# A macaron block in one program: latent attention scores computed twice without transposes, key norms read into an own tensor, new order of the feed-forward phases

## What is computed

```python
x = x + 0.5 * ffn(layernorm(x))     # two layers: local attention (8 heads of 64, windows of 64) + gated MLP
x = x + attn(layernorm(x))          # latent attention, 16 heads of 8, causal
x = x + 0.5 * ffn(layernorm(x))

# attn
q_lat = jnp.einsum('bqhd,hdl->bhql', q, k_eff)
attn = jnp.einsum('bhql,bkl->bhqk', q_lat, c_kv) / sqrt(hs)
attn = jnp.where(causal[None, None], attn, -jnp.inf)
attn = jax.nn.softmax(attn, axis=-1)

# one ffn layer
q = l2norm(q) * qs; k = l2norm(k) * ksc
q, k = rotary_xpos(q, k)
o = local_attention(q, k, v)
x = x + o @ wo
h = shift_token(x); h = layernorm(h) * lg + lb
a, g = jnp.split(h @ w1 + b1, 2, axis=-1)
x = x + (a * gelu(g)) @ w2 + b2
```

## Time and profile before

| | us |
|---|---|
| median of three runs | 2268.1 |
| the three runs | 2256.44 to 2269.57 |
| the profiled execution | 2281.34 |
| its span, first to last instruction | 2279.2 |
| busy: TensorE / VectorE / ScalarE / GpSimd | 1837.4 / 1444.4 / 1117.9 / 901.3 |

### The profile page before, as it was taken

One profiled execution on the slowest core, in us unless ns is written; L12 is line 12 of the kernel. 1 busy time (PEld: TensorE's weight loads), 2 busy tenths in 40 slices (PEclk: granted clock), 3 DMA queues, 4 the chain that ended last, 5 costly groups with the idle time before them and its releaser, 6 DMA issues. The chain is left out here.

```text
span 2279.2 us, 50236 instructions
## 1 busy us (share of the span) xinstructions
PE 1837.4 (81%) x20010; PEld 1120.2 (49%) x20074; DVE 1444.4 (63%) x2281; ACT 1117.9 (49%) x2070; POOL 901.3 (40%) x624
## 2 busy tenths in 40 slices
PE   1577888888888787799999996677788888887886
PEld 1344454544555454466666663344454544544543
DVE  2466766566665644688888885566666665555563
ACT  1134444354444433488888884234434444444342
POOL 2444444454444440222222222444544444444440
PEclk9888999899999989799999997789989898999899
DMA  3122223222222321000000000123322222233221
GB/s 123 36 59 61 69 70 93 62 60 66 68 68 73 84 60 29 1 2 1 2 1 2 1 1 1 46 60 87 76 60 60 61 73 60 70 90 77 64 65 42
DMA packets 60664, 118.84 MB, mean 52 GB/s; under 512 B 7519, under 2 KB 17939, under 8 KB 58259
## 3 DMA queue, kind: packets, MB, share of 16 engines
q1 hardware_dynamic: 60435, 115.64, 20.0%
HBM read 82.51 MB, written 3.74 MB: 38 GB/s over the span
## 5 line engine op out<-in xcount | busy, mean ns | idle before, releaser
L942 POOL TENSOR_TENSOR QK<-QK,SQ 128x1024 f32<-128x1024 f32 x128 | 298.3, 2352 | 190.6 <-DMA SQ<-norms_d 190.6
L782 DVE SCALAR_TENSOR_TENSOR TP<-bank,cols,tab 128x1024 f32<-128x1024 f32 x256 | 320.4, 1275 | 47.2 <-PE bank L447 34.5
L805 DVE TRANSPOSE_TENSOR_REDUCE MX<-bank 128x16 f32<-128x512 f32 x256 | 160.4, 684 | 264.6 <-PE bank L484 264.6
L936 POOL TENSOR_TENSOR QK<-TP 128x512 f32<-128x512 f32 x128 | 164.3, 1283 | 407.8 <-DVE TP L782 260.4
L1195 ACT ACTIVATE PL<-bank,NM 128x384 f32<-128x384 f32 (+3 forms) x512 | 255.5, 540 | 15.6 <-DVE NM L1275 12.7
L1275 DVE TENSOR_REDUCE NM<-bank 128x1 f32<-128x384 f32 (+3 forms) x352 | 217.7, 635 | 35.4 <-PE bank L1109 31.7
L475 PE MATMUL bank<-bandb,identb 128*128 128x512 bf16 x192 | 74.5, 510 | 180.8 <-POOL QK L942 178.0
L1118 PE MATMUL bank<-cst,PL 128*128 128x128 f32 x1280 | 200.0, 275 | 3.3 <-DVE PTL L1284 1.1
L639 ACT ACTIVATE SQ<-bank 128x512 f32<-128x512 f32 x128 | 76.5, 598 | 239.7 <-PE bank L447 239.7
L1104 PE MATMUL bank<-KL,QZL 128*128 128x384 f32 (+3 forms) x512 | 189.3, 422 | 2.3 <-DVE QZL L1232 2.3
L484 PEld LDWEIGHTS bank<-QK 32*64 32x64 f32 x8192 | 155.8, 162 | 40.8 <-issue 40.8
(11 more groups left out here) (171 smaller groups left out, 3777.1 us busy)
## 6 DMA issues: line engine op xcount, KB each, us to landing
SQ<-norms_d SPq DMA_DIRECT2D x128, 256.0 KB, 4.9
OT<-sums_d SPq DMA_DIRECT2D x128, 256.0 KB, 3.9
V<-V SPq DMA_DIRECT2D x32, 512.0 KB, 7.7
V<-V SPq DMA_DIRECT2D x32, 384.0 KB, 8.8
RB<-vars_d SPq DMA_DIRECT2D x32, 256.0 KB, 3.2
X<-in_L_attn_x SPq DMA_DIRECT2D x8, 256.0 KB, 4.4
out<-X SPq DMA_DIRECT2D x8, 256.0 KB, 8.5
wqkv_raw<-in_L_ffn_wqkv SPq DMA_DIRECT2D x1, 1536.0 KB
```

Source lines behind the costliest of these rows:

```text
L782: nc.vector.scalar_tensor_tensor(out=TP[:, o:o + 2, :], in0=BK[4 + z][:, :].unsqueeze(1).to_broadcast([P, 2, T]), scalar=q, in1=tab[:, e, ...
L805: last = nc.vector.tensor_reduce(MX[:, i, :], BK[i][:, :].rearrange("p (a b) -> p a b", b=32), AX_X, ALU.max, apply_transpose=True)
L936: nc.gpsimd.tensor_tensor(QK[:, m, 0, :], TP[:, 2, :], TP[:, 1, :], ALU.subtract)
L942: nc.gpsimd.tensor_tensor(QK[:, m, :, :], QK[:, m, :, :], SQ[:, m, 1, :].unsqueeze(1).to_broadcast([P, 2, T]), ALU.mult).then_inc(S["nr_ok ...
```

## The change

In both feed-forward phases: `norms` reads the norms back into a tensor of its own, `RB`, instead of the second half of `SQ`; `U` has one buffer instead of two; the lists of all engines are written in a new order.

```diff
@@ SyncE, norms
-                                sp.dma_start(SQ[32 * i:32 * i + 32, :, 1, :],
+                                sp.dma_start(RB[32 * i:32 * i + 32, :, :],
@@ ScalarE, square_b
-                                act.wait_ge(S["nr_ok"], 4 * (u - 1) + m + 1)
+                                act.wait_ge(S["ss_in"], u)
@@ TensorE, the new list
+                            run(project, n - 1, 1)
+                            run(add_max, n - 2, 0)
+                            run(hidden, n - 4, 0, 1, 7)
+                            run(hidden, n - 4, 0, 2, 6)
+                            run(project, n - 1, 2)
+                            run(scores, n - 2, 1)
+                            run(sums, n - 2, 0, 6)
+                            run(project, n - 1, 3)
+                            run(turn_max, n - 2, 1, 6)
+                            run(outward, n - 4, 7)
+                            run(add_max, n - 2, 1)
+                            run(norms, n - 1, 6)
+                            run(attend, n - 2, 0, 5)
+                            run(sums, n - 2, 1, 4)
...
+                            run(join, n - 2, 7)
+                            run(project, n, 0)
+                            run(scores, n - 1, 0)
@@ VectorE, the new list (its first half)
+                            run(gated, n - 4, 2, 6)
                             run(rotate, n - 1, 2, 1)
                             run(rotate, n - 1, 2, 0)
                             run(maxima, n - 2, 1)
+                            run(statistics, n)
+                            run(rotate, n - 1, 3, 1)
                             run(spread_max, n - 2, 1, 6)
-                            run(rotate, n - 1, 3, 1)
-                            run(gated, n - 4, 2, 7)
                             run(rotate, n - 1, 3, 0)
-                            run(clamp, n - 1, 7)
-                            run(attended, n - 2, 0, 6)
-                            run(attended, n - 2, 1, 4)
+                            run(outward, n - 4, 7)
+                            run(tokens, n)
+                            run(clamp, n - 1, 6)
+                            run(attended, n - 2, 0, 5)
```

```diff
+                RING = 3
+                AHEAD, QRING, KRING = 2, 3, 4
+                T_LAG = UN + 2
+                            pair = PAIR[place[0] % RING]
+                            claim(place[0] % RING, "ex_ok", m + 1)
+                            place[0] += 1
+                            lo, hi = DIAG_T[f]
+                            for e in range(2):
+                                nc.tensor.matmul(pair[:, e, lo:hi], identb[:, :],
+                                                 causaltb[:, :].unsqueeze(1).to_broadcast([P, (hi - lo) // P, P]),
+                                                 start=True, stop=False, skip_group_check=True)
+                            for j, o in FILLS_T[f]:
+                                N = T - j * P
+                                for e in range(2):
+                                    rows = slice(32 * (h0 + e), 32 * (h0 + e) + 32)
+                                    last = nc.tensor.matmul(pair[:, e, o:o + N],
+                                                            KS[rows, G % KRING, j * P:(j + 1) * P].bitcast(F32R),
+                                                            QC[rows, G % 2, j * P:T].bitcast(F32R),
+                                                            start=False, stop=True, skip_group_check=True)
...
+                            nc.scalar.activation(PTL[:, G % 2, h0:h0 + 2, f * T:f * T + WIDTH_T[f]],
+                                                 PAIR[at_t(m) % RING][:, :, 0:WIDTH_T[f]], ACT.Exp).then_inc(S["ex_ok"], 1)
...
+                            for i, o in FILLS[f]:
+                                last = nc.vector.tensor_reduce(NM[:, G % 2, i, 24 + 32 * h0:57 + 32 * h0:32],
+                                                               PAIR[at(m) % RING][:, :, o:o + (i + 1) * P],
+                                                               AX_X, ALU.max, negate=True)
...
+                            nc.vector.tensor_tensor(QC[:, G % 2, :].bitcast(F32R), BK[B_PREP][:, :], QS[:, G % QRING, :],
+                                                    ALU.add).then_inc(S["qc_ok"], 1)
...
+                            link(nc.gpsimd.tensor_scalar(HI[:, 0, :].bitcast(F32R), RAW[:, 0, :], low_q, None, ALU.mult))
...
+                            nc.gpsimd.tensor_tensor(QS[:, G % QRING, :].bitcast(F32R), RAW[:, 0, :], HI[:, 0, :],
+                                                    ALU.subtract).then_inc(S["qs_ok"], 1)
```

659 lines of the change are left out of this document (331 added, 328 removed).

## The result

The changed kernel takes **2350.08 us** (median of 3 runs, 2346.65 to 2368.57) against 2268.1: a ratio of 1.040, 95% interval 1.030 to 1.050. It is slower by 82 us; the forecast was 2286, and the measured time lies just beyond the upper end of its range of 2215 to 2350.

The account below looks back on a forecast made before the run. It took TensorE's own time to bound the latent attention and a 22.06 us norm chain the feed-forward units; -4 + 32 - 11 + 2 = +19 gave about 2300 us profiled, 2286 as median, range 2215 to 2350.

Parts of the forecast that it names:

- Latent attention, -4 us: Latent attention on TensorE: groups of 13.9 us, stage of 453 to 454 us against 457.4, so -4 us.
- rival 3: Latent attention: pairs of strips don't overlap, a group takes 16.2 us, +73, so 2359 us; chance 0.14.
- rival 1: Latent attention: the array changes cheaply, weights loaded under the masks; 2244 us, or 2167 with all of the change; chance 0.17.
- First layer, +32 us: Feed-forward first layer: the new order costs 2.3 us for each of 7 units per phase, +32 us.
- 1.6 to 1.8 us late: First layer: the next sequence's statistics, before the rotation, delay `CB`, `add_max` and the norm sums by 1.6 to 1.8 us.
- `Z` and `U` stand ahead of the clamp, which comes 0.7 late more: First layer: `Z` (1.5 us) and `U` (1.1 us) ahead of the clamp make it 0.7 us later.
- Second layer, 0: Feed-forward second layer: added TensorE work lies in idle time, so price 0, bounds -1 and +1 us per unit.
- Starts of the phases, -11: Start of each feed-forward phase: projections follow the first sequence's turning, -5.6 us, twice, -11.
- Drain, +2: End of each feed-forward phase: two `hidden` gates share bank 6, +1 us per phase, +2.
- Own tensor, 0: Feed-forward: `square_b` no longer waits for the multiplication, but ScalarE has nothing urgent behind it; price 0.
- Rival 2: Feed-forward phases: the new order pays, the +32 become 0 and 1 us per unit comes off, 2224 us; chance 0.13.
- Rival 4: Feed-forward phases: the clock stays low one more stretch, +2.5 us per unit, 2361 us at most, 2325 for half; chance 0.17.

Follow-up runs that it names:

- combined: Feed-forward phases of before with 24 added matmuls ahead of each unit's scores; after's latent attention with values at step end and added matmuls at its start: 2220.79 us.
- u_back: After, with the writing of `U`, its turning and the copies into `Z` moved behind the Newton step as in before, statistics left as in after: 2341.16 us.
- stats_back: After, with the next sequence's statistics, tokens' turning and copies moved behind the Newton step again, where before has them: 2330.33 us.
- mla_only: After's latent attention between before's feed-forward phases (their order, norms read into `SQ`, `U` in two buffers): 2299.24 us.
- sq_back: After, with the norms read back into the second half of the squares' tensor instead of a tensor of their own: 2352.13 us.
- warm: After, with 20 full-row bf16 matmuls that nothing reads added at the start of the latent attention: 2350.22 us.
- values_end: After, with the next sequence's values issued at the end of their step on TensorE instead of right behind the keys: 2341.59 us.
- warm_values: After, with 20 added matmuls at the start of the latent attention and the next sequence's values at the end of their step: 2327.95 us.
- merged: After, with the masks for maxima and probabilities set one behind the other, then both sets of strips, halving the array's changes: 2361.62 us.

## Why the prediction was wrong, by its own steps

**Latent attention, -4 us: wrong in sign, +14.** The prices of the fills held (0.65 and 0.53 against 0.66 and 0.56), the pairs of strips overlap (so rival 3 falls), the change of the array costs about 0.09 each way (so rival 1 falls), and the mean of the four groups of a sequence is 13.8 us without the values' wait, against 13.9 summed. Two steps failed. The first: the sum takes every group at the prices of full clock and has no term for a low stretch, and after was at half clock for 53 us at the start and 14 us later, before for 18. The second: the values were priced by their streaming alone although they follow the keys on the same bank, which is 1.2 us of wait per sequence. Taking that wait away gave back 15 us, wait and fall together; dense work at the start gave some 9 to 11 more. In `combined`, with both and full clock from 930.2 on, the stage runs 444 us from the first mask to the last turned output, where the sum has 451 (its 453 to 454 without the 2 us of projections), so the sum was also too high, by some 3 us in the groups and 4 in the ends of the stage. The rule that four strips lose part of their speedup (the Trainium skill, "TensorE: Matmul & The Clock Gate", Part 3), by which the stage would have been 16 us longer, is not seen with pairs: a fill of 512 columns costs 0.65 us, what it costs with its streams side by side. No run here has four strips of 512 columns side by side.

**First layer, +32 us: right in place and kind, too small; measured +53.** "1.6 to 1.8 us late" for the statistics: TensorE waits 0.96 us for `CB` at 340.71, and by `u_back` against `stats_back` the statistics are worth 9 us per phase, about 1.1 per unit. "`Z` and `U` stand ahead of the clamp, which comes 0.7 late more": this term was mis-sized; by after against `u_back` it is 12 us per phase, 1.5 per unit. `U` was priced at 1.1 us from a stretch where GpSimd was idle; now it is 2.96 us (343.32), since its writes fall on GpSimd's instructions. Each of the two slow writes ends 0.08 us behind one of them: at 344.54 and 345.77, GpSimd at 344.46 and 345.69. The other two, from 345.69 on with GpSimd idle, take 0.33 us each. It is so in the whole trace of after: 30 of the 96 writes of `U` take 1.22 to 1.31 us, each beside a `TENSOR_TENSOR` of GpSimd and ending 0.08 us behind it, and the 64 of 0.33 to 0.37 us overlap a `TENSOR_TENSOR` by 0.2 us at most. Beside a GpSimd instruction with one tensor as input, `TENSOR_SCALAR`, they are not slowed: 7 writes that lie wholly within one take 0.34 to 0.37 us. The clamp starts at 346.31, 2.6 us behind the end of the norm sums, and the way from norm sums to scores is 1.7 us longer. Moving `U` alone brought the writes back to 338 ns and that way back to 22.9. The Trainium skill says in "SBUF — State Buffer", "SBUF: two separate sides", that one pair of SBUF ports is shared by GpSimd and certain VectorE instructions, as a lock held for a whole instruction. The ends of the slow writes, 0.08 us behind GpSimd's, agree with it; the 7 writes that ran beside GpSimd's `TENSOR_SCALAR` in 0.34 to 0.37 us do not, so here the lock would have to depend on GpSimd's instruction too. That the writes of `U` are of those VectorE instructions no run here shows. No run took GpSimd's instructions away from `U`, only `U` from them. What is left of the +53, some 4 us per phase in `stats_back`, was not told apart.

**Second layer, 0:** +0.4 us in the second phase, +9.2 in the first, where before had shorter units (48 us) among those of 51; with `mla_only` (350.4 and 351.6) before's order takes 351 on average against after's 356. With the added matmuls it is +3.2 and +2.3 for seven units. So the order costs some 0.4 to 0.7 us per unit, inside the bounds of ±1.

**Starts of the phases, -11:** -6.6 and -5.4; right, and given back by `stats_back`. **Drain, +2:** in the first phase, from the last norm sums to the first turning of the latent input, -1.1 us (99.7 against 100.8). In the second, from the last norm sums to the end of the program, 99.3 us against 93.9, +5.4; all kernels with the new order show 99.3 to 101.9 there, those with before's order 93.9 to 96.8. The new order pays for it; which of its lines, no run here tells. **Own tensor, 0:** right (`sq_back`).

**Rival 2** (the order pays) is refuted by both layers. **Rival 4** (the clock stays low longer in the feed-forward phases) did not come: from the first to the last norm sums of a phase the granted clock is 0.91 and 0.89 in before and 0.91 and 0.92 in after. It did name the right agent, but for the other stage. Two sums of the prediction don't come out: half of rival 4 is 2286 + 38 = 2324, not 2325, and rivals 3 and 4 with a quarter to a half of the forecast's case are 0.41 to 0.51, not 0.36, so by its own terms slower was the likeliest. The rest of the +82 in the medians beyond the 69 of the traces is that before's profiled execution was 13 us above its own median.

## What to carry to other kernels

A stage that is bound by TensorE is forecast at full clock only if every wait in it is found first: two instructions on one bank with an eviction between them cost 1.2 us here, and then up to 14 us at half speed. Price a VectorE write from rows in which GpSimd does what it will do at the new place, since the same write was 0.34 or 1.22 us long. And where TensorE idles on a chain that can't be shortened, matmuls that nothing reads were worth 36 and 51 us here.

## What the runs showed that I had not expected

The clock stood at half for 38 us in which TensorE was busy 37.88 us (971 to 1009, masks and strips of 32 rows at the start of the stage), and it came back at 958.1 when full-row bf16 matmuls were put in the idle time ahead. The same values' wait of 1.2 us, once per sequence, brought a fall at one of seven places in after, at two in `mla_only` (1161.7 and 1339.2) and in `warm` (1180.0 and 1299.5), and the low stretches lasted 10 to 14 us each; which of the waits brings one changed from kernel to kernel. With the wait gone, in `values_end`, `warm_values` and `combined`, none came at these places. Not every fall needs this wait: `merged` has six between 1000 and 1400 us, with other waits in every group, and `warm` and `warm_values` fall near 980 where the maxima's turning waits. Why the clock stayed low at the stage's start, the strips of 32 rows or something else, was not told apart.
